# One kernel, one core: the shared expert's down product split into three terms of rounded halves, with rings of three and a new table of positions

## What is computed

```
h = ewma_both_ways(x) @ W.T + b                     # tokens: 16 x 750 rows of 256
h = h + two_selective_scans(layernorm(h))           # state-space layers with a class row
h = h + ffn(layernorm(h))                           # a mixture of experts
# ffn, for every row xf of 256:
sg = xf @ shared_gate_w.T                           # 256 -> 512
su = xf @ shared_up_w.T                             # 256 -> 512
shared_out = silu(sg) * su @ shared_down_w.T        # 512 -> 256
topk_idx, w = route(xf)                             # 4 of 16 experts, from 2 of 4 groups
routed = sum of w * (silu(xf @ gate_w) * (xf @ up_w)) @ down_w over the chosen experts
return shared_out + routed
```

## Time and profile before

| what | value |
| --- | --- |
| time, median of three runs | 1291.67 us (1291.62 to 1293.05) |
| the profiled execution's own time | 1292.31 us |
| its span | 1290.3 us |
| PE busy | 1174.1 us, 91% of the span |
| weight loads on PE busy | 1051.1 us, 81% |
| VectorE busy | 847.9 us, 66% |
| ScalarE busy | 655.4 us, 51% |
| POOL busy | 416.3 us, 32% |
| HBM traffic | 55 GB/s over the span |

### The profile page before, as it was taken

The page is one execution under the profiler, slowest core; times in us unless marked ns, Lnnn a source line. Parts: engine busy times, 40 slices in busy tenths (PEclk is TensorE's granted clock), DMA queues, the critical chain, the costliest instruction groups (busy, mean ns, idle before and its releaser), DMA issues. The chain is left out here.

```text
span 1290.3 us, 25188 instructions
## 1 busy us (share of the span) xinstructions
PE 1174.1 (91%) x7501; PEld 1051.1 (81%) x7501; DVE 847.9 (66%) x2259; ACT 655.4 (51%) x1297; POOL 416.3 (32%) x282
## 2 busy tenths in 40 slices
PE   3479877988999899998999899999999999999997
PEld 3447756867998789987988799978998899889997
DVE  5563887498557874888568964797388645644443
ACT  3645654573645555654655474656565443223332
POOL 2032254125221633134412623154303421253333
PEclk8757986998999999999999999999999999999999
DMA  4130021013122423122121323231312221243331
GB/s 126 33 89 14 27 66 41 26 45 81 43 50 43 101 55 54 38 60 75 31 62 31 91 55 54 42 97 42 59 38 50 74 38 39 56 111 53 54 52 18
DMA packets 88291, 71.50 MB, mean 55 GB/s; under 512 B 39671, under 2 KB 82848, under 8 KB 88168
## 3 DMA queue, kind: packets, MB, share of 16 engines
q1 hardware_dynamic: 58832, 43.30, 12.3%
q0 software_dynamic: 26832, 26.06, 12.2%
q10 hardware_dynamic: 2504, 0.55, 0.2%
HBM read 31.36 MB, written 39.34 MB: 55 GB/s over the span
## 5 line engine op out<-in xcount | busy, mean ns | idle before, releaser
L845 POOL DMA_INDIRECT out_dram<-block_rows,entry x99 | 156.4, 1580 | 330.4 <-ACT block_rows L1024 308.3
L1012 ACT ACTIVATE hid<-gu_ps 128x512 f32<-128x512 f32 (+1 forms) x195 | 114.8, 591 | 256.6 <-PE gu_ps L1770 181.6
L1770 PE MATMUL gu_ps<-gu_hi,bx_hi 128*128 x792 | 233.8, 295 | 2.8 <-issue 2.5
L1770 PE MATMUL gu_ps<-gu_lo,bx_hi 128*128 x792 | 224.0, 283 | 0.0
L1770 PE MATMUL gu_ps<-gu_hi,bx_lo 128*128 x792 | 223.7, 282 | 0.0
L826 POOL DMA_INDIRECT lists<-records,pos x96 | 129.4, 1348 | 197.2 <-DVE pos L1432 171.6
L1827 PE MATMUL d_ps<-down,hid 128*125 128x256 f32 x768 | 188.2, 390 | 0.0
L1827 PEld LDWEIGHTS d_ps<-down,hid 128*125 128x125 f32 x768 | 143.3, 194 | 19.9 <-issue 0.3
L1770 PEld LDWEIGHTS gu_ps<-gu_hi,bx_hi 128*128 128x128 f32 x792 | 150.2, 190 | 8.7 <-issue 7.8
L1770 PEld LDWEIGHTS gu_ps<-gu_hi,bx_lo 128*128 128x128 f32 x792 | 150.4, 190 | 0.8
L1770 PEld LDWEIGHTS gu_ps<-gu_lo,bx_hi 128*128 128x128 f32 x792 | 149.6, 189 | 0.0
(11 more groups left out here) (280 smaller groups left out, 2913.2 us busy)
## 6 DMA issues: line engine op xcount, KB each, us to landing
block_rows<-lists SPq DMA_DIRECT2D x99, 128.0 KB, 2.9
out_dram<-h SPq DMA_DIRECT2D x24, 500.0 KB
t<-rstd_scratch SPq DMA_DIRECT2D x21, 250.0 KB, 4.8
x_in<-in_x_dram SPq DMA_DIRECT2D x8, 375.0 KB, 7.6
zt<-in_x_dram SPq DMA_DIRECT2D x7, 375.0 KB, 3.6
entry<-lists SPq DMA_DIRECT2D x99, 8.0 KB, 2.6
out_dram<-block_rows,entry POOLq DMA_INDIRECT x99, 3.8
lists<-records,pos POOLq DMA_INDIRECT x96, 4.2
```

The source lines that it names most:

```text
L845: pool.indirect_dma_start(out=out_rows[0:there, :], out_offset=bass.IndirectOffsetOnAxis(entry[n % UE][:, ID:ID + 1].bitcast(U32), 0), in_ ...
L1012: inc(act.activation(hid[g % 4][:, 0:n], gu_ps[:, 2 * (g % 2), 0:n], ACT.Silu), "silu_done")
L1770: last = pe.matmul(gu_ps[:, 2 * (g % 2) + half, q * GH:(q + 1) * GH], a[n % 2][:, k, :], w[:, k, bass.ds(of, 1), half * GH:(half + 1) * GH ...
```

## The change

Six things change.

- `down` becomes `down_hi` and `down_lo`, both fp32r. The preparation, which did only ScalarE's copy for it, now has VectorE's subtraction as well, twice.
- `shared_hi` on ScalarE rounds the hidden values of an S slot, last in the slot's tick g+2. `shared_lo` on VectorE subtracts, last in its tick g+2. They use the buffers `hid_hi` and `hid_lo` that only blocks used.
- `shared_down` stays in tick g+3, waits for `s_lo` where it waited for `hid_done`, and does three fp32r matmuls where it did one float32 matmul.
- The ring of `hid` goes from four buffers to three; a buffer that an S slot held is free for the next silu when `shared_lo` of the slot three back has run (before: when `shared_down` of the slot four back had run).
- U and UO go from 4 to 3.
- `CHAIN`, `EARLY` and `PREPARE` have other numbers in some 60 rows, mostly by half a tick to one tick and a half.

```diff
-    ("residual", 1, dict(DVE=-4.5)),
-    ("class_row", 0, dict(PE=-7.0, DVE=-7.5)),
+    ("residual", 1, dict(DVE=-6.0)),
+    ("class_row", 0, dict(PE=-8.0, DVE=-7.5)),
...
-    U, UE, UO = 4, 12, 4
+    U, UE, UO = 3, 12, 3
...
-        down = sb("down", [P, M, D])
+        down_hi, down_lo = (sb(f"down_{s}", [P, M, D], F32R) for s in ("hi", "lo"))
...
-        hid_t = sb("hid", [P, 4, 512])
-        hid = [hid_t[:, n, :] for n in range(4)]
+        NH = 3
+        hid_t = sb("hid", [P, NH, 512])
+        hid = [hid_t[:, n, :] for n in range(NH)]
...
-            return down[:, :, (n % KD) * P:(n % KD + 1) * P], None
+            return [w[:, :, (n % KD) * P:(n % KD + 1) * P] for w in (down_hi, down_lo)]
...
-                was = slot(g - 4)
+                was = slot(g - NH)
                 if was[0] == "S":
-                    wait(act, "down_mm", done(g - 4))
+                    wait(act, "s_lo", s_count(*was[1:]))
...
+            def shared_hi(pair, n, g):
+                wait(act, "hid_done", done(g))
+                wait(act, "down_mm", done(g - 2))
+                inc(act.activation(hid_hi[g % 2][:, 0:TT], hid[g % NH][:, 0:TT], ACT.Copy), "s_hi")
...
+            def shared_lo(pair, n, g):
+                wait(dve, "s_hi", s_count(pair, n))
+                inc(dve.tensor_tensor(hid_lo[g % 2][:, 0:TT], hid[g % NH][:, 0:TT],
+                                      hid_hi[g % 2][:, 0:TT].bitcast(F32), ALU.subtract), "s_lo")
...
             def shared_down(pair, n, g):
                 m = n % M
-                wait(pe, "hid_done", done(g))
+                wait(pe, "s_lo", s_count(pair, n))
...
-                    last = pe.matmul(d_ps[0:TP, j, :], hid[g % 4][:, tc], down[:, m, :],
-                                     start=(m == 0 and j % 2 == 0), stop=(m == M - 1), skip_group_check=True)
+                    for c, (a, w) in enumerate(((hid_hi, down_hi), (hid_hi, down_lo), (hid_lo, down_hi))):
+                        last = pe.matmul(d_ps[0:TP, j, :], a[g % 2][:, tc], w[:, m, :],
+                                         start=(m == 0 and j % 2 == 0 and c == 0), stop=(m == M - 1 and c == 2),
+                                         skip_group_check=True)
```

More of the change, by code:

```diff
@@ L21 @@
 CHAIN = (
-    ("ewma", 0, dict(SP=-32.5, DVE=-33.5, POOL=-29.0, ACT=-29.5)),
+    ("ewma", 0, dict(SP=-32.0, DVE=-33.0, POOL=-28.5, ACT=-29.0)),
     ("ewma_back", 0, dict(DVE=-32.0)),
@@ L32 @@
     ("pre", (0, 0), dict(PE=-19.5, DVE=-19.5)),
-    ("ln1_part", 0, dict(DVE=-24.5, POOL=-27.0)),
-    ("split", (0, 0), dict(ACT=-14.5, DVE=-14.0)),
+    ("ln1_part", 0, dict(DVE=-24.5, POOL=-26.0)),
+    ("split", (0, 0), dict(ACT=-14.0, DVE=-14.0)),
+    ("pre", (0, 1), dict(PE=-19.0, DVE=-18.5)),
     ("tok", 4, dict(PE=-25.0, DVE=-25.0)),
-    ("pre", (0, 1), dict(PE=-19.0, DVE=-18.5)),
-    ("carry", 0, dict(PE=-13.0, DVE=-13.5)),
+    ("carry", 0, dict(PE=-13.0, DVE=-14.0)),
     ("ln1_stats", 0, dict(DVE=-23.0, POOL=-24.5)),
@@ L40 @@
     ("spread", 0, dict(SP=-21.5)),
[L41 to L45, removed]
+    ("rstd_row", 0, dict(PE=-23.3, ACT=-23.7)),
+    ("split", (0, 1), dict(ACT=-13.5, DVE=-13.5)),
+    ("rstd_row", 1, dict(PE=-22.4, ACT=-23.3)),
+    ("rstd_row", 2, dict(PE=-22.0, ACT=-17.5)),
+    ("ln1_part", 1, dict(DVE=-23.5, POOL=-22.5)),
     ("rstd_t", 0, dict(PE=-22.0, ACT=-21.5)),
@@ L73 @@
     ("ln2_norm", 1, dict(DVE=-2.0, ACT=-1.5)),
-    ("residual", 4, dict(DVE=-1.5)),
+    ("residual", 4, dict(DVE=-2.0)),
+    ("x2t", (0, 0), dict(PE=-3.0, ACT=-3.0, DVE=-2.5)),
     ("y", (2, 0), dict(PE=-1.5, DVE=-1.5)),
[L76 to L79, removed]
     ("x2t", (0, 1), dict(PE=-2.5, ACT=-2.5, DVE=-2.5)),
@@ L108 @@
     ("list", 0, dict(POOL=13.5)),
-    ("route_pick", 0, dict(DVE=7.5)),
-    ("list", 1, dict(POOL=14.0)),
+    ("list", 1, dict(POOL=13.5)),
     ("list", 2, dict(POOL=15.0)),
     ("route_marks", 2, dict(DVE=12.5)),
+    ("list", 3, dict(POOL=15.0)),
+    ("route_pick", 0, dict(DVE=7.5)),
+    ("list", 4, dict(POOL=16.5)),
     ("place_sum", 0, dict(DVE=10.0)),
-    ("list", 3, dict(POOL=16.5)),
-    ("list", 4, dict(POOL=17.5)),
-    ("route_top", 2, dict(DVE=11.5)),
     ("list", 5, dict(POOL=17.5)),
@@ L119 @@
     ("list", 6, dict(POOL=18.0)),
-    ("list", 8, dict(POOL=18.0)),
+    ("list", 8, dict(POOL=19.0)),
     ("list", 9, dict(POOL=19.5)),
+    ("route_top", 2, dict(DVE=11.5)),
+    ("list", 10, dict(POOL=20.5)),
     ("table", 0, dict(DVE=14.0)),
-    ("list", 10, dict(POOL=21.5)),
     ("table", 1, dict(DVE=15.0)),
@@ L152 @@
     (0, "list", 9): dict(POOL=17.5),
-    (0, "list", 10): dict(POOL=16.5),
+    (0, "list", 10): dict(POOL=13.5),
     (1, "y", (2, 1)): dict(PE=-1.5, DVE=-1.5),
@@ L172 @@
     (0, "x2t", (0, 0)): dict(ACT=-3.5),
-    (2, "list", 11): dict(POOL=18.5),
+    (2, "list", 11): dict(POOL=15.5),
     (1, "list", 9): dict(POOL=18.5),
@@ L224 @@
     (0, "route_top", 1): dict(DVE=9.5),
+    (0, "tok", 5): dict(PE=-24.0, DVE=-24.0),
+    (0, "ssm_log", 0): dict(ACT=-16.5, DVE=-15.5),
+    (2, "ln1_part", 0): dict(POOL=-27.5),
+    (1, "place_sum", 0): dict(DVE=12.0),
+    (1, "ln1_part", 0): dict(POOL=-25.0),
+    (1, "ln1_stats", 0): dict(POOL=-23.5),
 }
@@ L238 @@
     (-19.5, "fold", 3),
[L239 removed]
+    (-13.9, "fold", 4),
     (-0.6, "routed", 0),
[L241 removed]
+    (6.4, "routed", 1),
     (-12.4, "shared", 1),
@@ L1052, in _ @@
                     block_hi(slot(g - 2)[1], g - 2)
+                elif slot(g - 2)[0] == "S":
+                    shared_hi(*slot(g - 2)[1:], g - 2)
         @block.vector
@@ L1574, in _ @@
                     block_lo(slot(g - 2)[1], g - 2)
+                elif slot(g - 2)[0] == "S":
+                    shared_lo(*slot(g - 2)[1:], g - 2)
         @block.tensor
@@ L1813, in block_hidden @@
                 for m in range(4):
-                    last = pe.transpose(ch("bh", 0, n)[:, m * P:(m + 1) * P], hid[g % 4][:, m * P:(m + 1) * P], ident[:])
+                    last = pe.transpose(ch("bh", 0, n)[:, m * P:(m + 1) * P], hid[g % NH][:, m * P:(m + 1) * P], ident[:])
                 inc(last, "bh_mm")
```

61 lines of the change are left out of this document (31 added, 30 removed).

## The result

The changed kernel takes 1317.33 us (median of four runs, 1315.42 to 1320.32); the kernel before, measured beside it, took 1291.64. The ratio is 1.0204, with a 95% interval from 1.0178 to 1.0229: slower by 26 us. Forecast were 1275 us and a range up to 1293.

A forecast was written before the change was run, and what follows sets the result against it. PE was taken as the bound over two thirds of the span, VectorE in parts of the startup; -27.8 + 4.1 + 4.2 + 2.9 = -16.6 us gave 1275 us against a median of 1291.7, range 1262 to 1293.

The forecast's parts named there:

- PE's price: Shared down product of an S slot on PE: 1.44 us for 1.73, saving 0.29 a slot, 27.8 us for 96.
- The rival with 0.107 us a matmul: New product's matmuls on PE follow each other faster: 1.28 us a slot, 43 us less, 1249 us; chance 0.03.
- two kinds of stretch: Steady periods: VectorE busy 44.3 of 50 us in the third group's stretch, 55.9 of 90 in the rest.
- I cost the subtractions there at nothing: Third groups of pairs three to seven, 20 slots: VectorE's 2.4 us fit into 5.7 us free.
- The startup: Stretches from 110 to 350 us, 14 slots: PE's saving of 4.1 us lost, half of VectorE's 8.4 us exposed, 4.2.
- its two losses: PE's saving taken as lost: 4.1 us in 14 startup slots, 2.9 us in 20 third-group slots.
- VectorE becomes the bound: Subtractions in N full stretches cost 0.60 us each and lose their slot's saving: 1294 to 1303 us; chance 0.15.
- The rings: Buffers cut from four to three: copies and row loads have time enough, costed at nothing unless POOL is over two blocks late.
- The new wait: `shared_down` in tick g+3 waits for VectorE's last instruction of tick g+2: costed at nothing unless chain work sits inside.
- The moved steps: New table positions, mainly VectorE's averaging scan behind the layer's scan: 9 us saved at best or lost at worst, taken as 0.
- Gain given back: Loop of silu, copy and subtraction takes about 0.3 us from each slot: 1291 us, within 2.6 us; chance 0.07.
- The clock: PE's granted clock in startup windows: 0.85 of full in the first, 1.00 from the second on.

The follow-up runs named there:

- pe_two: The kernel before with eight fp32r matmuls (two terms) for the four float32 ones in each shared slot, nothing added on VectorE or ScalarE: 1263.34 us, 0.9784 of before.
- pe_only: The kernel before with twelve fp32r matmuls for the four float32 ones in each shared slot, no copies or subtractions in the slots: 1291.22 us, 0.9948 of before.
- before_sub: The kernel before, float32 product and tables kept, with 96 unused subtractions added on VectorE: 1319.35 us, 1.0214 of before.
- no_lo: The changed kernel without VectorE's 96 subtractions, PE and silu waiting for ScalarE's copy instead: 1279.85 us, 0.9924 of before.
- no_hi: The changed kernel without ScalarE's 96 copies, the subtraction waiting for silu's product itself: 1318.77 us, 1.0205 of before.
- rings_four: The changed kernel with hid, U and UO at four buffers and `down_lo` left out: 1317.68 us, 1.0145 of before; measured again 1314.00 us, 1.0168.
- the exchanges of tables: `CHAIN`, `EARLY` and `PREPARE` swapped: changed kernel with before's 1335.84 us, 1.0292 of before; kernel before with the changed kernel's 1293.39 us, 0.9958.
- the short runs: POOL's additions and subtractions of the averages cut to 32 columns in pairs 1 to 7: changed kernel 1.0020 of before, kernel before 0.9880.

## Why the prediction was wrong

**PE's price was right.** Since the starts next to a product of another shape shift as well, I compare a longer row with the same neighbours: from the second matmul ahead of the product to the sixth behind it, before and in the changed kernel.

```profile
984.20 0.39 PE L1743 MATMUL gu_ps<-x_lo,up_hi 128*128 128x500 f32 x1
...
984.65 1.89 PE L1827 MATMUL d_ps<-down,hid 128*125 128x256 f32 x8
...
987.50 0.39 PE L1743 MATMUL gu_ps<-x_hi,gate_lo 128*128 128x500 f32 x1
```

```profile
863.70 0.39 PE L1764 MATMUL gu_ps<-x_lo,up_hi 128*128 128x500 f32 x1
...
864.15 0.28 PE L1849 MATMUL d_ps<-down_hi,hid_hi 128*125 128x256 f32 x1
864.27 0.28 PE L1849 MATMUL d_ps<-down_lo,hid_hi 128*125 128x256 f32 x1
...
865.57 0.39 PE L1764 MATMUL gu_ps<-x_hi,gate_hi 128*128 128x500 f32 x1
...
866.70 0.39 PE L1764 MATMUL gu_ps<-x_hi,gate_lo 128*128 128x500 f32 x1
```

It was 3.30 us and is 3.00, and other slots with like neighbours give 0.30 to 0.32 us too. The new product costs 1.42 us where I had 1.44, its starts lie 0.12 us apart, and PE is saved some 29 us, not 27.8. In pe_two the same row takes 2.53 us, 0.47 less again or 45 us for all slots. The rival with 0.107 us a matmul is refuted.

**The step that failed is the first**: "over two thirds of the span PE is the bound, and a microsecond less of PE work there is worth nearly a microsecond". I read it from a busy share of 97% over whole periods. pe_only shows 6.7 us for those 29, and pe_two 28 for 29 + 45. In the table, pe_only gains 1.2 us over the five steady pairs from pair 2 to pair 7, where I had 17.4 less 2.9. I had even set down that the rows hide two kinds of stretch, and then priced only 34 of 96 slots by the second kind. A busy share says how much work there is, not whose next instruction the others wait for: with PE short of work by 4.7 us a period and VectorE by 5.7 us in the third group, the two were nearly tied, and a saving on PE ran into VectorE at once.

**"I cost the subtractions there at nothing"** failed too. The subtractions didn't fill the 5.7 us in which VectorE was free in the third group's stretch: one there costs 0.42 us. The likely reason is that these were waits for data (1.8 us of them for the class row), which other work can't simply fill. In the steady pairs (from pair 2 to pair 7) before_sub's shift grows by 16.4 us, where I had nothing. **The startup** has the same fault in size: 4.2 us for half of the subtractions, where before_sub had 10.4 by pair 2. Without its VectorE term, the forecast was 1275 less 4.2; no_lo, the kernel without that term, is at 1279.85. The error of the sum is thus first the subtractions, 4.2 us forecast against 28 to 37 measured, and then PE's saving, 20.8 us forecast after its two losses against 6.7 in pe_only. no_lo is 10 us below before, but with the new tables, worth 5 us in before.

**The rival "VectorE becomes the bound"** named the mechanism, and with N of 34 to 44 slots 1294 to 1303 us. Its price for the subtractions, 0.60 us each or 20 to 26 us in all, comes close to before_sub's 28. It fell short by the other term: it let PE's saving stand in all slots outside, 15 to 18 us, where pe_only kept 6.7.

**What held.** ScalarE's copies cost nothing that can be measured (no_hi). The rings cost nothing, or up to 8 us. The new wait on PE is not needed for a loss of this size (before_sub lacks it), but in the first two pairs PE waited 19.1 us there, and what that costs isn't shown. The moved steps I had at 0; the exchanges of tables show a gain. "Gain given back" by the loop of silu, copy and subtraction is refuted: without the copy (no_hi) and with silu hardly waiting for the subtraction (rings_four) the loss remains.

**The clock.** I had read 1.00 "from the second on". That held from 250 to 290 us only; from 290 to 310 us the trace of before has 0.74. The changed kernel's mean is lower than before's, 0.939 against 0.951, and no run holds the clock fixed. before_sub, at 0.947 with PE's busy time at before's 1174.1 us, has the whole loss, so a lower clock on PE's work isn't needed for it; what it adds in the changed kernel is not shown.

**What stays open.** How 26 us divide between VectorE's own work and its time beside POOL: the short runs give 18 and 8, if the two simply add; in before_sub, with as large a loss, the prolonged instructions took only 4 us more than in before. And the parts don't add up to the whole: before_sub and pe_only make +28 and -7, the new tables -5 to -11, and the change is at +26, so 10 us or more come from the parts together, the rings (up to 8) and the waits of PE and silu for the subtraction among them.

## What to carry to other kernels

A bound is what gives time back when its work is taken away, and a high busy share doesn't show that. Where two engines stand at 94% and 89% of a stretch, ask of each added instruction in which stretch it falls: the same 0.68 us cost nothing in ticks 2 to 5 and 0.42 us in ticks 15 to 18. Here work moved from the fuller engine to the second fullest, and that would have paid only where the first set the pace. Long waits on a third engine (here 100 us for rings) are no loss until a run without them says so. And a matmul's price is best read over a row with the same neighbours in both kernels: up to the very next start, the old and the new product look nearly alike, 1.54 and 1.51 us at the median of the steady pairs.

No run here that computes the whole result beats before with the new product in it. The kernel before with the new tables does beat it, at 0.9958 of before (0.9938 to 0.9979), and with the additions on VectorE too, at 0.9960.

## What the hardware showed that I had not expected

VectorE instructions with both inputs in SBUF took up to 3.42 us instead of 0.93 (`states`, in before), and 3.05 instead of 0.68 (`hid_lo`, in before_sub), while POOL instructions ran, most often its additions of 750 columns. Some with a single input from SBUF were prolonged too. Those with an input in PSUM stayed within 0.03 us of their median in each of the sixteen traces that I summed. Cutting POOL's two such instructions to 32 columns gave 15.5 us in before, 1.2% of the time, with POOL busy only 32% of the span. The prolonged instructions took 13 us less in it; how much of the gain is that, and how much the averages' earlier arrival, isn't told apart.
